# Causal mask on VectorE, a later load of the next tokens, and a reordered drain, in a fused cross-attention, MLA attention and feed-forward kernel

## The reference, cut to what matters

```
x = x + cross_attention(layernorm(x), ctx, mask)            # stage x
x = x + attention(layernorm(x), ...)                        # stage m
x = x + ffn(layernorm(x), ...)                              # stage f

attention:  q = rmsnorm(x wq_a + b) wq_b + b    -> q_nope, q_pe;   q_nope <- q_nope wkv_b[:, :128]
            kv, k_pe = x wkv_a + b;  rope on q_pe and k_pe;  kv = rmsnorm(kv)
            scores = (q_nope kv^T + q_pe k_pe^T) / sqrt(192), causal
            out = softmax(scores) kv wkv_b[:, 128:] wo + b
```

## Time and profile before

| | before |
|---|---|
| median of 3 runs | 1105.37 us (1103.42 to 1109.07) |
| profiled execution: its own time / its span | 1104.65 / 1102.8 us |
| mean granted TensorE clock | 0.974 |
| PE busy | 1029.5 us, 93% of the span, 7617 matmuls |
| DVE busy | 500.9 us, 45% |
| ACT busy | 327.4 us, 30% |
| POOL busy | 295.4 us, 27% |
| chain that ended last | PE 80%, issue 7%, DVE 4%, DMA 3%, POOL 3%, SPq 2%, ACT 1% |

### The profile page before, as it was taken

How to read it: one execution, slowest core, us unless ns; L and a number is a source line. 1 busy time by engine, 2 the same in 40 slices (tenths; PEclk the granted TensorE clock), 3 DMA queues, 4 the chain that set the end, 5 groups by cost and what they waited for, 6 DMA issues and landing times.

```text
span 1102.8 us, 19174 instructions
## 1 busy us (share of the span) xinstructions
PE 1029.5 (93%) x7617; PEld 839.0 (76%) x7617; DVE 500.9 (45%) x946; ACT 327.4 (30%) x598; POOL 295.4 (27%) x347
## 2 busy tenths in 40 slices
PE   6999999799985999859998798999999999999997
PEld 3677786588864888748886687888888888888886
DVE  3666565455544455335554467353431152234114
ACT  3555554222221222212221133443132222223220
POOL 2434372411112111131111220242143214213412
PEclk9999999899998999979999799999999999999999
DMA  9999963300033001320014051430001002000101
GB/s 359 413 419 391 406 212 88 68 20 21 21 68 91 17 19 29 81 67 20 21 49 96 10 168 44 138 111 1 1 12 66 1 1 77 1 1 1 39 1 39
DMA packets 41532, 101.60 MB, mean 92 GB/s; under 512 B 7465, under 2 KB 11844, under 8 KB 36964
## 3 DMA queue, kind: packets, MB, share of 16 engines
q1 hardware_dynamic: 39716, 96.82, 26.2%
q10 hardware_dynamic: 1728, 3.54, 0.8%
HBM read 74.65 MB, written 17.30 MB: 83 GB/s over the span
## 4 chain that ended last, share of the span: by engine, by line
PE 80%; issue 7%; DVE 4%; DMA 3%; POOL 3%; SPq 2%; ACT 1%; DVEq 0%; POOLq 0%; ACTq 0%
PE b_z L44 7%; PE b_z L46 7%; PE b_z L45 7%; PE b_turn L44 4%; PE b_turn L45 4%; PE b_turn L46 4%; PE b_score L44 4%; PE b_score L46 4%; PE b_score L45 4%; PE b_prob L46 4%; PE b_prob L44 4%; PE b_prob L45 4%; PE b_read L45 3%; PE b_read L44 3%; PE b_read L46 3%
## 5 line engine op out<-in xcount | busy, mean ns | idle before, releaser
L1540 POOL TENSOR_TENSOR f_hT_lo<-f_h,f_hT_hi 128x512 fp32r<-128x512 f32 x64 | 82.0, 1282 | 243.1 <-ACT f_hT_hi L1595 233.0
L1656 DVE TENSOR_TENSOR f_h<-f_h 128x512 f32<-128x512 f32 x64 | 45.4, 710 | 152.9 <-ACT f_h L1588 152.9
L44 PE MATMUL b_z<-m_zT_lo,m_wq_hi 128*128 128x512 f32 x192 | 78.4, 408 | 34.2 <-ACT m_qT L883 34.2
L45 PE MATMUL b_z<-m_zT_hi,m_wq_lo 128*128 128x512 f32 x192 | 77.3, 402 | 0.0
L46 PE MATMUL b_z<-m_zT_hi,m_wq_hi 128*128 128x512 f32 x192 | 77.1, 402 | 0.0
L44 PEld LDWEIGHTS b_z<-m_zT_lo,m_wq_hi 128*128 128x128 f32 x192 | 37.8, 197 | 43.8 <-ACT m_qT L883 35.5
L831 POOL TENSOR_TENSOR m_sc<-m_sc,m_causal 128x512 f32<-128x512 f32 x16 | 21.1, 1316 | 186.4 <-DVE m_sc L978 186.4
L820 POOL TENSOR_TENSOR m_qpe<-m_qpe,m_swapped 128x512 f32<-128x512 f32 x32 | 41.1, 1285 | 110.6 <-DMA m_swapped<-m_by_sin 110.6
L883 ACT ACTIVATE m_qT<-b_z,m_q_bias 128x512 f32<-128x512 f32 x64 | 43.5, 685 | 69.1 <-PE b_z L46 64.2
L44 PE MATMUL b_score<-m_wvo_lo,m_oT_hi 128*128 128x512 f32 x128 | 52.9, 413 | 10.2 <-DVE m_x L1017 7.6
L1595 ACT CAST f_hT_hi<-f_h 128x512 fp32r<-128x512 f32 x64 | 39.8, 622 | 54.3 <-DVE f_h L1656 54.3
(11 more groups left out here) (278 smaller groups left out, 2858.8 us busy)
## 6 DMA issues: line engine op xcount, KB each, us to landing
x_ctx_in<-ctx_rows_dram SPq DMA_DIRECT2D x16, 1024.0 KB, 14.6
x_ctxT<-ctx_turned_dram SPq DMA_DIRECT2D x15, 1024.0 KB, 14.7
m_swapped<-m_by_sin SPq DMA_DIRECT2D x128, 64.0 KB, 2.0
m_raw<-attn_raw_dram SPq DMA_DIRECT2D x6, 768.0 KB, 10.9
m_z_in<-z_scratch SPq DMA_DIRECT2D x16, 288.0 KB, 4.0
x_x_all<-x_dram SPq DMA_DIRECT2D x16, 256.0 KB, 15.0
m_x<-x_scratch SPq DMA_DIRECT2D x16, 256.0 KB, 4.7
x_scratch<-m_x SPq DMA_DIRECT2D x16, 256.0 KB, 3.8
```

The lines of the kernel that those rows point to most:

```text
L44: nc.tensor.matmul(out, lh, rl, start=first, stop=False)
L45: nc.tensor.matmul(out, ll, rh, start=False, stop=False)
L1540: q.tensor_tensor(hT_lo[k % 6][:], h[:, k % 2], hT_hi[k % 6][:].bitcast(F32), ALU.subtract).then_inc(s["h_lo"], 1)
L1656: v.tensor_tensor(h[:, k % 2], h[:, k % 2], h[:, k % 2], ALU.mult).then_inc(s["squared"], 1)
```

## The change

It has three parts.

1. `mask(u)` moves from GpSimd to VectorE. The same addition on the same views is issued by VectorE in slot u, behind `turn_scores(u)` and `out(u-1, 0)`. GpSimd did it in slot u+1 as its first instruction. In the hand-written end both masks leave GpSimd's list; that of the last unit stands on VectorE behind `split_weights(1)`.
2. `load_z(g+1)` is issued by SyncE in n = 2 instead of n = 0, behind `swap(u)`. The load of `z_read` in the last group stays in n = 0.
3. In the end written by hand VectorE does `out(U-1, 0)` ahead of `turn_scores(U)`, and `probs(U)` ahead of `square(0,0)` and `residual(U-1, 3)`.

```diff
@@ SyncE, slot
             swap(u)
-            if n == 0:
+            if n == (2 if has_next(g) else 0):
                 sp.wait_ge(s["kv_lo"], g + 1)
                 sp.wait_ge(s["k_turned1"], g + 1)
                 if has_next(g):
@@ GpSimd
-        def mask(u):
-
-            pool.wait_ge(s["s_turned"], 2 * (u + 1))
-            own = sc[:].rearrange("p (b w n) -> p b w n", b=2, w=3)[:, :, 0::2]
-            q.tensor_tensor(own, own, causal[:].unsqueeze(1).unsqueeze(1).broadcast_to([P, 2, 2, HU * QB]),
-                            ALU.add).then_inc(s["masked"], 1)
...
         def slot(g, n, u):
-            if runs(g, n, 1):
-                mask(u - 1)
             rope_add(u, 0)
@@ VectorE
+        def mask(u):
+
+            dve.wait_ge(s["s_turned"], 2 * (u + 1))
+            own = sc[:].rearrange("p (b w n) -> p b w n", b=2, w=3)[:, :, 0::2]
+            v.tensor_tensor(own, own, causal[:].unsqueeze(1).unsqueeze(1).broadcast_to([P, 2, 2, HU * QB]),
+                            ALU.add).then_inc(s["masked"], 1)
...
             turn_scores(u)
             if runs(g, n, 1):
                 out(u - 1, 0)
+            mask(u)
             if n == 0:
                 values(g)
@@ program, GpSimd
-            m["mask"](U - 1)
             f["rsqrt"](0, 0)
             m["rope_add"](U, 0)
             m["norm"](U - 1)
             m["rope_add"](U, 1)
-            m["mask"](U)
             m["norm"](U)
@@ program, VectorE
             m["out"](U - 1, 1)
+            m["out"](U - 1, 0)
             m["turn_scores"](U)
-            m["out"](U - 1, 0)
             f["split_weights"](1)
+            m["mask"](U)
             m["residual"](G, U - 1, 0)
             m["shift"](U)
...
             m["turn_probs"](U)
             f["split_weights"](3)
+            m["probs"](U)
             f["square"](0, 0)
             m["residual"](G, U - 1, 3)
-            m["probs"](U)
             f["square"](0, 1)
```

More of the change, by code:

```diff
@@ L852, in groups @@
             slots(pool, slot)
-        return dict(groups=groups, rope_add=rope_add, mask=mask, norm=norm)
+        return dict(groups=groups, rope_add=rope_add, norm=norm)
     def scalar(act):
@@ L1072, in vector @@
         return dict(latent=latent, groups=groups, rotate=rotate, invert=invert, probs=probs, out=out,
-                    turn_scores=turn_scores, turn_probs=turn_probs, shift=shift, residual=residual, tables=tables)
+                    turn_scores=turn_scores, mask=mask, turn_probs=turn_probs, shift=shift, residual=residual, tables=tables)
     def tensor(pe):
```

## The result

The changed kernel takes 1059.36 us (median of 4 runs, 1056.47 to 1061.05) against 1105.09 us for the kernel before (4 runs): a ratio of 0.9578, 95% interval 0.9545 to 0.9612. The forecast was 1057.0 us, with a range of 1044 to 1072.

A forecast was written before the change was run, and what follows sets the result against it. TensorE's waits and the low clock behind them were taken as the loss; 27.6 + 9.4 + 6.3 + 5.1 = 48.4 us off 1104.65 gives 1056.3 profiled, 1057.0 as median. Own range 1050 to 1064, wider 1044 to 1072.

The forecast's parts named there:

- n = 2, 27.6 us: Slots n = 2, groups 1 to 3: m_qT waits go, waits near 3 us stay; 27.6 of 42.4 us excess goes.
- n = 1, 9.4 us: Slots n = 1, groups 1 to 3: the swap comes sooner without z loads; 9.4 of 11.4 us excess goes.
- The mask itself: VectorE's queue: the mask takes near 0.7 us and adds 0.6 us to the queue.
- z in n = 2: SyncE's z loads behind swap(u) land by +26 us; TensorE needs them at +42, so nothing waits.
- Group 0, 6.3 us: Group 0: m_wvo_lo wait falls from 6.1 to 1.6 us and the clock stays up; 6.3 us gained.
- The drain, 5.1 us: Hand-written end: reordering saves 1.9 and 1.7 us of waits and 1.5 us of low clock; 5.1 us.
- the remainder is gone: Rival, n = 2: all 42.4 us of excess go, 1042 us; chance 0.07.
- The remainder is bigger: Rival, n = 2: 2.4 us more wait and 1.3 us more low clock per slot, 1068 us; chance 0.18.
- The mask is slow: Rival: the mask takes 1.26 us on VectorE, eleven slots lose about 0.5 us each, 1063 us; chance 0.08.
- it doesn't do what it says: Rival, n = 2: something else holds exp and only the other parts pay, 1085 us; chance 0.04.
- z at TensorE: Rival: late z loads hold turn_latent; slipping 34 us gives about 1111 us; chance 0.03, including back to the old time.

The follow-up runs named there:

- bias_behind_norm: The changed kernel with GpSimd's bias_x1(g) moved to n = 2 behind norm(u-1); 1047.96 us, ratio 0.9487.
- swap_first: pool_mask_all with the first half of the swap issued by SyncE ahead of the x1 loads in n = 2; 1041.56 us, ratio 0.9437.
- swap_first_dve: bias_behind_norm (mask on VectorE) with the first half of the swap ahead of the x1 loads in n = 2; 1042.68 us, ratio 0.9446.
- z_only: The kernel before with only the z load moved to n = 2; 1092.00 us, ratio 0.9878.
- bias_split: The changed kernel with bias_x1's first tile ahead of norm, the other three behind rope_add 1, all in n = 2; 1046.58 us, ratio 0.9473.
- probs_late: The changed kernel with probs(U) back behind square(0,0) and residual(U-1, 3) in the drain; 1061.62 us, ratio 0.9626.
- mask_only: The kernel before with only the mask moved to VectorE; 1079.45 us, ratio 0.9772.
- pool_mask_all: The changed kernel but with the mask on GpSimd and bias_x1 in n = 2 behind norm; 1046.55 us, ratio 0.9471.

## Why the prediction was right, point by point

- **n = 2, 27.6 us.** The three slots lost 28.4 us (42.4 to 14.1 of excess). The waits left are 3.26, 3.06 and 3.61 us, 9.9 in sum (forecast 9.4). `bias_behind_norm` shows their cause to be the one named. The price of low clock was 1.9 us behind two of them and 0.3 behind the third, where 1.8 had been put to each. That the sum fits is in part luck: group by group the forecast was 3.1, 3.6 and 2.7 us, up to 0.9 off, because the bias adds started 9.78, 9.58 and 10.13 us behind `turn_scores` where the rows of before had 9.74, 10.29 and 9.39. `invert` was done 2.0 us before `norm` could start in group 1 (at 343.20 and 345.24), where 1.1 had been worked out.
- **n = 1, 9.4 us.** 9.6 us: 0.38 and 0.37 us are left in groups 1 and 2 (forecast 0.4), 1.05 in group 3 (forecast 1.2). `swap_first` against `swap_first_dve` (27.35 and 27.67) shows that it is the mask's.
- **The mask itself.** 0.67 us on VectorE, 0.6 us from its start to the next instruction (forecast 0.7 and 0.6).
- **z in n = 2.** Nothing waits for z: no list of TensorE's waits has one for `turn_latent`. In group 1 of the kernel after z is issued from 348.6 to 352.4 and the first `turn_latent` runs at 376.7. `z_only` gives what was expected of it.
- **Group 0, 6.3 us.** The term that was mis-sized: 3.9 us. The prediction had `probs(0)` free of neighbours. In the kernel after it meets the bias adds of group 0:

```profile
207.03 5.67 POOL L825 TENSOR_TENSOR m_x<-m_x,m_wo_b 128x512 f32<-128x512 f32 x4
```

```profile
207.26 1.85 DVE L929 TENSOR_TENSOR m_pT_lo<-m_pT,m_pT_hi 128x768 fp32r<-128x768 f32 x1 [1.39 <-ACT m_pT_hi L880]
```

  1.85 us instead of 0.96; TensorE waits 2.4 us instead of 1.6, and its clock falls (0.93 over the slot), where the forecast had kept it full. In `bias_split`, where no bias add runs there, the low part takes 0.96 us, the wait is 1.5 us and the slot 20.71 us: 6.35 us gained, the forecast's number. The bias adds alone cost 0.9 us of wait, and the clock the other 1.6. The clock's part varies between executions: `probs_late` has the same instructions here, the low part takes 1.81 us and TensorE waits 2.3 us, but the clock stays at 1.00 and the slot takes 21.58 us, 5.5 us gained. The prediction weighed the rule of the Trainium skill ("SBUF — State Buffer", "Who interferes with whom") for n = 2, where it hardly counted, and missed it here, where the trace agrees with it.
- **The drain, 5.1 us.** 436.98 to 431.85: 5.1 us. The waits were sized right (3.6 us forecast, 3.8 measured as below), but that the total fits to a tenth is luck with the clock. The four kernels with the old order have tails of 435.66 us (full clock behind both waits), 436.98 (before: low behind the first), 436.73 (`mask_only`: low behind the second) and 439.27 us (`z_only`: low behind both). So the new order gives back 3.8 us of waits and between 0 and 3.6 us of clock.
- **What was not foreseen:** 1.1 us lost in the other slots and ahead of the first, 0.6 of it in n = 3 of group 0, where a wait of TensorE with no releaser ("issue") is 0.8 us instead of 0.2. It comes and goes between all these kernels. 28.4 + 9.6 + 3.9 + 5.1 - 1.1 = 45.9 us, the difference of the spans.

The rivals: "the remainder is gone" is what `swap_first_dve` has, but by two further edits. "The remainder is bigger" would have left 26 us of excess in n = 2, and 14.1 are left; its swap behind the x1 loads is real (VectorE waits 4.27 us for it in the kernel after), but it set the time only once `norm` had been freed from the bias. "The mask is slow", "it doesn't do what it says" and "z at TensorE" are refuted by the mask's 0.67 us, by `mask_only` and by `z_only`.

## What to carry to other kernels

When an engine's instruction waits 20 us for a DMA, look at what stands behind it in its queue before moving work to another engine: putting the wait behind the urgent work gave more (36.8 us, one edit) than moving one urgent instruction to another engine (25.7 us). The same holds for DMA queues: a small exchange on the critical chain belongs ahead of bulk loads (5.0 us between `pool_mask_all` and `swap_first`). When a large wait goes, follow the same queue for what is late next; here it was worked out from the rows of before, to half a microsecond in the sum and 0.9 us in a single slot, and it named the next edit. Look too at whether a wait was followed by the low clock: between executions of the same instructions that alone moved a slot by up to 1.6 us.

## What the runs showed of the hardware

The length of a wait alone did not tell whether TensorE's clock fell. In the kernel after, behind waits of 2.4, 3.3 and 3.6 us:

```profile
209.86:213.00 3.14, 3.14 (x50) 2.38 (x50) 1.14 (x2) 0.59 (x1) 2.84 (x3) 0.75 0.00 0
350.33:354.00 3.67, 3.67 (x11) 2.95 (x12) 0.45 (x1) 0.00 (x0) 0.67 (x1) 0.64 1.03 227
585.39:589.00 3.61, 3.61 (x16) 2.98 (x17) 1.82 (x4) 0.00 (x0) 0.38 (x1) 1.00 0.00 0
```

The longest of the three kept the full clock, the shortest did not. The same wait can go either way: the 2.35 us wait of the first line is 2.32 us in `probs_late`, and the 4 us behind it ran at 1.00; the 1.74 us wait on `m_pT_lo` was followed by 1.00 in the kernel before and by 0.72 in `probs_late`. Why was not tried.

VectorE's low part of the probabilities takes 0.96 us alone and 1.36 (`bias_split`), 1.70 (n = 1 of group 1 of the kernel after) or 1.85 us beside an addition on GpSimd. The four bias adds grow from 4.92 to 5.67 us where they meet it.
